# GpSimd waits for attention at eight places within the gathers of a step

## The reference

```python
# layer 0: max over the first S = 25 neighbours of each node, by index
h = maximum(layernorm(x), 0)
idx = the 25 lowest neighbour indices of each row of adj
agg = h[idx].max(over the 25)            # and 0, if a node has 25 neighbours or fewer
x = x + relu(concat(h, agg) @ W0 + b0)
# layer 1: attention over all neighbours
h = maximum(layernorm(x), 0)
hidden = h @ W1.T
s = leaky_relu(hidden @ a[0] (per row) + hidden @ a[1] (per column), 0.2)
s = where(adj > 0, s, s - 1e12)
x = x + softmax(s) @ hidden + bias
```

## Time and profile before

| | |
|---|---|
| median of 3 runs | 5939.51 us (5937.73 to 5965.89) |
| the profiled execution | 5909.85 us, its span 5908.0 us |
| busy: GpSimd | 3060.1 us (52%) |
| busy: TensorE | 2655.1 us (45%) |
| busy: VectorE | 2621.4 us (44%) |
| busy: ScalarE | 1563.1 us (26%) |
| DMA queue of the gathers (q0) | 419.64 MB, 24.0% of 16 engines' time |
| DMA queue of SyncE (q1) | 378.64 MB, 20.0% |
| chain of waits that ended last | unknown releaser 28%, VectorE 25%, issue 20%, TensorE 14%, ScalarE 9% |

### The profile page before, as it was taken

How to read it: one execution, slowest core, us unless ns; L and a number is a source line. 1 busy time by engine, 2 the same in 40 slices (tenths; PEclk the granted TensorE clock), 3 DMA queues, 4 the chain that set the end, 5 groups by cost and what they waited for, 6 DMA issues and landing times.

```text
span 5908.0 us, 37877 instructions
## 1 busy us (share of the span) xinstructions
PE 2655.1 (45%) x8782; PEld 1602.9 (27%) x8782; DVE 2621.4 (44%) x6725; ACT 1563.1 (26%) x1745; POOL 3060.1 (52%) x3204
## 2 busy tenths in 40 slices
PE   1222244454454444454444534444534454344469
PEld 0111122232222223222222322222312232222246
DVE  4444444553344544444533445434445344354432
ACT  3111122232232222232222322322323223222135
POOL 5566654545546555546544555545564455554530
PEclk6555566666666767666666666666767666566789
DMA  7344455544445454555444454544554444444420
GB/s 257 120 139 132 137 154 150 171 145 151 135 140 174 148 158 138 154 149 176 147 151 136 152 160 149 160 136 150 164 159 146 154 137 147 148 145 145 128 94 26
DMA packets 477222, 865.97 MB, mean 147 GB/s; under 512 B 308298, under 2 KB 309204, under 8 KB 456660
## 3 DMA queue, kind: packets, MB, share of 16 engines
q0 software_dynamic: 153600, 419.64, 24.0%
q1 hardware_dynamic: 305140, 378.64, 20.0%
q10 hardware_dynamic: 18432, 67.12, 3.1%
HBM read 690.98 MB, written 119.54 MB: 137 GB/s over the span
## 4 chain that ended last, share of the span: by engine, by line
another core or an unknown queue 28%; DVE 25%; issue 20%; PE 14%; ACT 9%; DVEq 1%; SPq 1%; POOL 1%; DMA 1%; ACTq 1%; POOLq 0%
DVE highest L880 8%; PE acc L1296 5%; ACT nm_t L531 3%; DVE top L814 3%; DVE key L820 3%; DVE lin L904 2%; PE bank L1229 2%; ACT wgt L567 2%; DVE stat L741 1%; PE bank L1209 1%; PE bank L1246 1%; DVEq L920 1%; ACT pen L561 1%; PE acc L1252 1%
## 5 line engine op out<-in xcount | busy, mean ns | idle before, releaser
L486 POOL DMA_INDIRECT near<-table_dram,idx x3200 | 3059.9, 956 | 2610.0 <-DVE agg L885 1424.8
L1296 PE MATMUL acc<-hid,wgt 128*128 (+1 forms) x4096 | 1159.0, 434 | 887.6 <-ACT wgt L567 493.7
L1296 PEld LDWEIGHTS acc<-hid,wgt 128*128 128x128 f32 x4096 | 870.6, 218 | 1077.7 <-issue 882.8
L880 DVE TENSOR_TENSOR highest<-near,highest 128x512 f32<-128x512 f32 x1280 | 889.8, 695 | 193.7 <-DVE highest L880 99.5
L896 DVE SCALAR_TENSOR_TENSOR x_q<-bank,x_q 128x256 f32<-128x256 f32 x128 | 54.1, 423 | 1740.4 <-PE bank L1231 1384.0
L567 ACT ACTIVATE wgt<-pen,a_slope 128x512 f32<-128x512 f32 x448 | 304.2, 679 | 1266.8 <-remote 900.1
L1229 PE MATMUL bank<-w_sb,h_t 128*128 128x256 f32 x1024 | 407.7, 567 | 425.8 <-ACT h_t L657 267.6
L531 ACT ACTIVATE nm_t<-adj_i,big_c 128x2048 bf16<-128x2048 int32 x128 | 499.8, 3955 | 4.6 <-DMA adj_i<-in_adj_dram 4.6
L814 DVE MAX8 top<-key 128x8 f32<-128x256 f32 (+1 forms) x1024 | 362.1, 387 | 306.6 <-remote 193.1
L1238 PE MATMUL acc<-cst,wgt 128*128 128x128 f32 x248 | 61.0, 428 | 926.1 <-ACT wgt L542 926.1
L1229 PEld LDWEIGHTS bank<-w_sb,h_t 128*128 128x128 f32 x1024 | 275.6, 282 | 515.8 <-ACT h_t L657 290.9
(11 more groups left out here) (148 smaller groups left out, 2209.9 us busy)
## 6 DMA issues: line engine op xcount, KB each, us to landing
adj_i<-in_adj_dram SPq DMA_DIRECT2D x128, 1024.0 KB
nmask_dram<-nm_t ACTq DMA_DIRECT2D x128, 512.0 KB
nm_q<-nmask_dram SPq DMA_DIRECT2D x29, 2048.0 KB
near<-table_dram,idx POOLq DMA_INDIRECT x3200
h_q<-table_dram SPq DMA_DIRECT2D x32, 512.0 KB
x_q<-in_x_dram SPq DMA_DIRECT2D x32, 512.0 KB
xmid_dram<-x_q SPq DMA_DIRECT2D x32, 512.0 KB
o_q<-xmid_dram SPq DMA_DIRECT2D x32, 512.0 KB
```

Of the source, the lines that this page charges most:

```text
L486: pool.indirect_dma_start(out=near[:, t % 2, k, :], out_offset=None, in_=table, in_offset=bass.IndirectOffsetOnAxis(ap=idx[:, t, k:k + 1], ...
L880: nc.vector.tensor_tensor(highest[:, :], pair(k), highest[:, :], ALU.max).then_inc(mx_step, 1)
L1296: mm = nc.tensor.matmul(acc[:, t, 0:C + 1], wgt_part(j)[:, t * P:(t + 1) * P], hid[:, bass.ds(batch * NJ + j, 1), 0:C + 1].rearrange("p a ...
```

## The change

A function `attention` is called before each gather `k` of each tile `t`. At eight pairs of tile and gather GpSimd first waits for a semaphore of the attention that the other engines are doing: before gathers 8, 12 and 20 of tile 0 for chunks 0 to 3, 0 to 5 and 0 to 7 of the previous step's quad (`a - 1`; tile 0 is gathered while the previous step is still under way); before gather 6 of tile 2 for `hid` of the quad `s - 1` and before its gather 22 for the first two penalties; before gathers 8, 16 and 22 of tile 3 for chunk 0, 0 to 1 and 0 to 2 of this step's quad. `wgt_used` starts at 4 and rises by one for each `j`. The waits of tile 0 come with a stage of their own, `attended`, from step 5 on, those of tiles 2 and 3 from step 4 on. Nothing else is changed; in the last quad (step 31) there are no new waits.

```diff
--- before.py
+++ after.py
@@ -64,6 +64,7 @@
     "gather": (0, QUADS - 2),
     "project": (1, QUADS - 2),
     "attend": (LAG, QUADS - 2),
+    "attended": (LAG + 1, QUADS - 2),
 }
 
 
@@ -472,6 +473,24 @@
             pool.wait_ge(first_out, 16 * QB)
             pool.wait_ge(fill_out, 16)
 
+            def attention(s, stages, t, k):
+
+                a = s - LAG
+                if "attended" in stages and (t, k) in ((0, 8), (0, 12), (0, 20)):
+                    chunks = {(0, 8): 4, (0, 12): 6, (0, 20): NJ // 2}[t, k]
+                    pool.wait_ge(wgt_used, NJ * (a - 1) + 2 * chunks + 4)
+                    pool.nop(nofuse=True)
+                if "attend" in stages and (t, k) == (2, 6):
+                    pool.wait_ge(hid_made, s)
+                    pool.nop(nofuse=True)
+                if "attend" in stages and (t, k) == (2, 22):
+                    pool.wait_ge(pen_made, NJ * a + 2)
+                    pool.nop(nofuse=True)
+                if "attend" in stages and (t, k) in ((3, 8), (3, 16), (3, 22)):
+                    chunks = {(3, 8): 1, (3, 16): 2, (3, 22): 3}[t, k]
+                    pool.wait_ge(wgt_used, NJ * a + 2 * chunks + 4)
+                    pool.nop(nofuse=True)
+
             def step(s, lo, stages):
                 if "gather" not in stages:
                     return
@@ -483,6 +502,7 @@
                     pool.wait_ge(agg_made, T * s + t + 1)
                     pool.nop(nofuse=True)
                     for k in range(S):
+                        attention(s, stages, t, k)
                         pool.indirect_dma_start(
                             out=near[:, t % 2, k, :], out_offset=None, in_=table,
                             in_offset=bass.IndirectOffsetOnAxis(ap=idx[:, t, k:k + 1], axis=0),
```

## The result

The changed kernel takes 5772.9 us (median of 4 runs, 5742.37 to 5784.86), the kernel before beside it 5942.41 us (4 runs, 5937.73 to 5965.89): a ratio of 0.970, interval 0.967 to 0.973. The forecast was 5470. The sign was right, and the gain of 169.5 us is a little over a third of the 468 us expected. The profiled execution took 5742.37 us, 167.5 us less than that of before.

The account below looks back on a forecast made before the run. No engine is near full; attention waits for signals delayed by gather bursts. A step of 180.55 us falls to 160, less 2.5 for set-up: 18 x 26 = 468 us saved, giving 5470; range 5255 to 5970.

Parts of the forecast that it names:

- Tile 2, both waits 0: Waits before gathers 6 and 22 of tile 2: met or costing about 1 us each, so counted as 0.
- Tile 3: Waits before its gathers 8, 16, 22: pauses 1, 9 and at most 3 us; attention wins ten; landing near +90.
- Tile 0: Next step's tile 0: 13 us pause at gather 12, chunk 7 at about +129, tile ending at +135.
- Tile 1: Next step's tile 1, without a new wait: gathered from +135 to +167, in place of +139.9 to +171.
- The step's end: From chunk 7 to the end of the step: kept at 30.7 us, giving a step of 160 us.
- a sign of being wrong: Step's end: an early chunk 7 with over 36 us to the end would show gathers pushed into the end.
- The slower rival: Gathers pushed into the step's end lengthen it 12 to 16 us; about 6095 us in all; chance 0.18.
- The +87.4: Attention in step 15 of the kernel before: the weights of chunk 1 said to be done at +87.4 us.
- The first rival: The pauses at the gathers buy nothing: chunk 7 stays at +147.6, time 5940 us within 0.5%; chance 0.10.

Follow-up runs that it names:

- e1_tail8: The changed kernel plus a ninth wait, before gather 8 of tile 1, for the layernorm statistics of the step before; 5697.03 us, ratio 0.957.
- e9_before: The kernel before, unchanged, run again for its own trace while the machine was in its quick condition; 4272.87 us (one run).
- e5_tail16: The changed kernel plus a ninth wait, for the layernorm statistics, before gather 16 of tile 1; 4270.25 us, ratio 1.000 to a kernel before of 4270 us.
- e6_tile0: The changed kernel with only the three waits of tile 0 left; 4270.0 us, ratio 1.000 to a kernel before of 4270 us.
- e7_no2: The changed kernel without the two waits of tile 2 (gathers 6 and 22); 4269.61 us, ratio 0.9994 to a kernel before of 4270 us.
- e8_drain8: The kernel before with GpSimd waiting, before gathers 8 and 16 of every tile, until the tile's earlier gathers have landed; 5024.13 us, ratio 1.177.
- e15_all8: The changed kernel with one wait in tile 0, before gather 8 for all 8 chunks, in place of three; 4375.43 us, ratio 1.024.

## Why the prediction was wrong in size

Point by point, by the prediction's own steps.

- **Tile 2, both waits 0.** Gather 6 was met; gather 22 paused about 3 us, where at most 2 were allowed for. Little hangs on it.
- **Tile 3.** A pause of 9 us at gather 16 was forecast; it was 2.9. The weights of chunk 1 came at a median of +62.0 instead of +82.8, and the pause that stands before them is the one at gather 8 (2.75 us). Tile 3 lands at +83.7, not +90. Attention won 20 us here, and not 10. A short pause early in the burst did more than its length.
- **Tile 0.** `x_q` of tile 2 forecast at +105: 2740.21, +103.4. The pause at gather 12 forecast as 13 us: 16, and 19 in the median. Chunk 7 forecast at +129: +126.0. Tile 0 ends at +137 (forecast +135). All pauses come to some 28 us a step, where 27 were forecast.
- **Tile 1**, forecast +135 to +167: +137 to +168. GpSimd was to become level with the chain, and its gap before the next tile 2 to shrink from 17 us to a few. It stayed at 17 to 18 (18.4 in step 15): GpSimd had slack, as the step had not become short.
- **The step's end.** Here is the failed step, in the prediction's words: "It still covers the step's end as now, so I keep 30.7 us for it: +129 + 30.7 = +160." Chunk 7 was early, and the stretch behind it took 47.5 us. 21.6 us were won and 16.8 given back. The prediction had named this as a sign of being wrong: an early chunk 7 with more than 36 us from it to the end.
- **The slower rival** named that mechanism, at 12 to 16 us, but as an alternative to the early chunk 7, to set in only if chunk 7 came later than +140. It came together with it.
- **A reading.** The +87.4 given for the weights of chunk 1 is the end of its products; the weights stand at +82.8 in the kernel before, which the forecast for tile 3 used. Nothing was added up from the other number.

The residual chain does not take a fixed time. It comes to a stand under the later part of a burst and goes on when that ends, and in the kernel before the burst had already run for 20 us when the last residual came. "As now" was wrong for that reason: with chunk 7 earlier by 20 us and tile 1 in place, the whole burst lies over the chain instead of a third of it. And the sum was at hand. The `shift` of step 15 came 7 us after tile 1's burst, which starts at 2837.73 and takes 31 us. The prediction had that burst end at +167. Add 7 and the step is 174, 6.5 us less than before; times 26, 169 us, and the time 5770. Measured: 174.34 and 5772.9. This is worked out with the result known. That the burst holds the chain is shown by e1_tail8, which paused GpSimd there and had the end at 21.4 us, and by step 5 of the changed kernel, with 17.0; that the step would end 7 us behind it is read off both kernels.

The prediction was right, as far as the runs go, about what bounds the kernel: not an engine, but the other engines held back while gathers are issued. It took the gap for one of attention alone. Every chain under a burst has it, and a step has 125 us of bursts. Moving them from one chain onto another gained only where a chain had slack. The first rival, pauses that buy nothing, did not come under this condition, and the Trainium skill's rule that TensorE and ScalarE never wait on others (SBUF — State Buffer, section "SBUF: two separate sides") was no reason to expect it: ScalarE stood idle for 18.38 us before a copy whose product had ended 15.9 us earlier. Under the other condition the rival's outcome came, 1.000, but because nothing was late there. What the rule speaks of, though, is access to SBUF, and no access was seen to be slow: an activation into `wgt` takes 679 ns on average in both kernels with late signals and in e9_before.

**What stays open.** What differs between the two conditions of the machine wasn't found. The DMA engines are no slower in the first: q0 spent 24.0% of 16 x 5908 us on 153600 packets, 0.148 us each, against 35.3% of 16 x 4271.1, 0.157 us. Whether e5_tail16, e6_tile0, e7_no2, e8_drain8 and e15_all8 help under late signals was not seen, since none of them ran there. Nor was the mechanism that holds an engine shown, only when it does. For each run the span and the granted clock are on record, so each was recorded as it ran; whether the recording has a part in the late condition was not tried. And the chain of statistics in the kernel before was read as held by the burst from its distance to it; no pause was tried there in that kernel.

## What to carry to other kernels

When a change moves a burst or the work beside it, don't carry a stretch over as a constant: look over many steps at what its end keeps a fixed distance to (here 7 us behind the last gather of tile 1, step after step), and forecast that. A pause that helps one chain pushes the rest of the burst onto the next one, so follow the paused work round to where it collides; three short pauses in tile 3 (0.974) were nearly all of the gain here. And measure the kernel before again beside every comparison: the change gave 3% where it took 5940 us and nothing where it took 4270.

## What was unexpected of the hardware

The same kernel took 5951 and 4270 us on one chip within half an hour, its runs within 1% of each other each time. In the loop that is 54.6 us of each step of 180.5, and what the traces show of it are engines that stand idle while GpSimd issues indirect DMAs, up to 25 us at a time, though what they wait for is done (in that case 21.8 us before). In the late condition the delay of a single signal, one VectorE instruction to the next, was 9.5 us under a burst, 1.2 us just after it and 0.5 us some 6 us later. Early in a burst there is no delay (in the kernel before none of 1203 in the first 15 us), and after a pause of 2 us VectorE's chain ran nearly without one again (step 5 of the changed kernel). Instructions that wait for no semaphore are held too, for up to 1.75 us. The lateness follows the number of gathers and not their bytes (a quarter of the bytes: 5943.91 us; a third of the gathers: 3969.95 us). That last time is below the 4270 us of the quick condition, because the gathers themselves are the bound there.
